# Second attention of a two-layer transformer program: the remainder of the output is subtracted on GpSimd instead of VectorE

## What is computed

```python
q = (x @ wq).reshape(b, s, H, HD); k = ...; v = ...        # H = 32, HD = 16
q = _apply_rotary(q, cos, sin); k = _apply_rotary(k, cos, sin)
scores = jnp.einsum('bqhd,bkhd->bhqk', q, k) * scale
scores = jnp.where(causal[None, None], scores, jnp.finfo(scores.dtype).min)
probs = jax.nn.softmax(scores, axis=-1)
out = jnp.einsum('bhqk,bkhd->bqhd', probs, v).reshape(b, s, d)
return out @ wo
```

## Time and profile before

| | |
|---|---|
| median of three timed runs | 2025.14 us (2019.7 to 2030.21) |
| the profiled execution | 2017.43 us, of it 2015.3 us span |
| TensorE busy | 1927.3 us, 96% of the span |
| VectorE busy | 1525.7 us, 76% |
| ScalarE busy | 882.8 us, 44% |
| GpSimd busy | 885.6 us, 44% |
| second attention, its even course | about 1650 to 1830 us of the span |

### The profile page before, as it was taken

The page is one execution under the profiler, slowest core; times in us unless marked ns, Lnnn a source line. Parts: engine busy times, 40 slices in busy tenths (PEclk is TensorE's granted clock), DMA queues, the critical chain, the costliest instruction groups (busy, mean ns, idle before and its releaser), DMA issues.

```text
span 2015.3 us, 41251 instructions
## 1 busy us (share of the span) xinstructions
PE 1927.3 (96%) x13992; PEld 1685.2 (84%) x13992; DVE 1525.7 (76%) x2354; ACT 882.8 (44%) x2235; POOL 885.6 (44%) x840
## 2 busy tenths in 40 slices
PE   8999979999999999999999999988999989998998
PEld 3688869999999999999999999976889877777776
DVE  2577657787777888777788887877888468778886
ACT  1233334444444444444444444445654445556432
POOL 0123354444444444444444443453685556666111
PEclk9999989999999999999999999999999989999999
DMA  9567751111111111111111111412487754443121
GB/s 336 174 206 240 230 166 47 47 47 47 47 47 47 47 46 44 44 44 45 42 47 47 47 47 42 140 42 63 133 244 222 228 172 127 131 130 98 38 63 58
DMA packets 197085, 207.20 MB, mean 103 GB/s; under 512 B 18554, under 2 KB 167930, under 8 KB 195996
## 3 DMA queue, kind: packets, MB, share of 16 engines
q1 hardware_dynamic: 196156, 205.53, 33.1%
q10 hardware_dynamic: 864, 0.79, 0.1%
HBM read 126.43 MB, written 71.43 MB: 98 GB/s over the span
## 4 chain that ended last, share of the span: by engine, by line
PE 67%; issue 13%; DVE 10%; SPq 3%; POOL 3%; DMA 2%; ACT 1%; DVEq 0%; POOLq 0%; ACTq 0%
PE ps L1028 17%; PE ps L989 17%; PE ps L1003 7%; PE ps L1017 4%; PE ps L1040 4%; SPq L1301 3%; PE ps L1012 3%; PE ps L2543 2%; POOL k_rot L564 2%; DVE f_inv_sum L1984 2%; PE ps L2507 2%; PE ps L1793 2%; PE ps L2114 2%; DVE f_neg_max L1979 2%; PE ps L2085 1%
## 5 line engine op out<-in xcount | busy, mean ns | idle before, releaser
L1028 PE MATMUL ps<-wo,ot 128*128 (+1 forms) x1536 | 388.9, 402 | 0.1
L1028 PEld LDWEIGHTS ps<-wo,ot 128*128 128x128 f32 x1536 | 282.0, 190 | 60.5 <-issue 1.2
L989 PE MATMUL ps<-ht_hi,wq 128*128 (+1 forms) x2048 | 287.5, 283 | 3.9 <-DVE q_swap L862 3.9
L989 PEld LDWEIGHTS ps<-ht_hi,wq 128*128 128x128 f32 x2048 | 268.5, 192 | 9.8 <-DVE q_swap L862 4.1
L789 ACT ACTIVATE prob<-ps,neg_max 128x128 f32<-128x128 f32 (+1 forms) x512 | 208.3, 421 | 130.2 <-DVE neg_max L869 105.2
L946 POOL TENSOR_TENSOR q_rot<-q_rot,q_swap 128x512 f32<-128x512 f32 x128 | 165.1, 1290 | 201.3 <-DVE q_swap L862 196.8
L796 ACT ACTIVATE pt<-ps 128x512 fp32r<-128x512 f32 x192 | 107.9, 598 | 301.7 <-PE ps L1040 301.7
L941 POOL TENSOR_TENSOR prob<-prob,inv_sum 128x512 f32<-128x512 f32 x64 | 66.6, 1040 | 288.2 <-DVE inv_sum L878 288.2
L1979 DVE TENSOR_REDUCE f_neg_max<-ps 128x4 f32<-128x1024 f32 (+1 forms) x128 | 119.7, 954 | 67.1 <-PE ps L2085 60.4
L989 PE MATMUL ps<-ht_lo,wq 128*128 (+1 forms) x1024 | 165.0, 283 | 0.0
L1003 PE MATMUL ps<-pt,vv 128*128 128x512 f32 x576 | 146.0, 397 | 8.6 <-issue 7.7
(11 more groups left out here) (247 smaller groups left out, 4238.0 us busy)
## 6 DMA issues: line engine op xcount, KB each, us to landing
stack_dram<-e_part SPq DMA_DIRECT2D x192, 128.0 KB, 2.4
v_dram<-v_part SPq DMA_DIRECT2D x32, 512.0 KB, 5.6
k_dram<-k_part SPq DMA_DIRECT2D x64, 256.0 KB, 2.7
kk<-k_dram SPq DMA_DIRECT2D x128, 128.0 KB, 2.1
vv<-v_dram SPq DMA_DIRECT2D x128, 128.0 KB, 2.1
wmod<-in_wmod SPq DMA_DIRECT2D x12, 1024.0 KB, 11.5
f_q<-stack_dram SPq DMA_DIRECT2D x62, 192.0 KB, 2.6
f_k<-stack_dram SPq DMA_DIRECT2D x124, 96.0 KB, 2.5
```

What stands on the lines that cost most here:

```text
L989: mm = nc.tensor.matmul(ps_q[j][:, e], w[:, c:c + HD0], r[:, bass.ds(u % B, 1), k].rearrange("p o s -> p (o s)"), start=(n == 0), stop=(n ...
L1028: mm = nc.tensor.matmul(ps_y[j][:], o[:, j, h * P:(h + 1) * P], w[:, bass.ds(at + h * D, D)], start=(n == 0), stop=(n == len(passes) - 1))
```

## The change

The function `low` moves from the program of VectorE to that of GpSimd. On GpSimd it stands behind `cut` and `add_blocks` of the same odd step; on VectorE it stood ahead of `output`. What it waits for and what it announces stay the same, and so do the data.

```diff
@@ -1986,17 +1986,9 @@
             dst = keep.ot1_raw[:, bass.ds(w, 1)].rearrange("p o s -> p (o s)")
             nc.vector.tensor_tensor(dst, ps_o[i][:, 0], inv_sum[i][:], ALU.mult).then_inc(o_out, 1)
 
-        def low(w):
-
-            dve.wait_ge(o_hi, w + 1)
-            hi, lo, raw = (t[:, bass.ds(w, 1)].rearrange("p o s -> p (o s)") for t in (*keep.ot1, keep.ot1_raw))
-            nc.vector.tensor_tensor(lo, raw, f32(hi), ALU.subtract).then_inc(o_split, 1)
-
         def step(v, slot, at):
             if at < U - 2:
                 maxima(v + 2, slot % 2)
-            if 5 <= at and slot % 2:
-                low((v - 5) // 2)
             if 2 <= at and slot % 2:
                 output((v - 3) // 2, (slot + 1) // 2 % 2)
             if at >= TAIL:
@@ -2013,9 +2005,7 @@
             dve.wait_ge(keep.qk_out[n], 192 * B)
         dve.wait_ge(keep.v_kept, 16 * B + 16)
         rest(dve, step)
-        low(PAIRS - 2)
         output(PAIRS - 1, 1)
-        low(PAIRS - 1)
 
     def scalar(act, side):
         def negated(u, slot):
@@ -2066,12 +2056,22 @@
             pool.wait_ge(p_cut, 2 * u + 2)
             nc.gpsimd.tensor_tensor(both[slot % 2][:], prob0[slot % 2][:, :, P:S], prob1[slot % 2][:], ALU.add).then_inc(p_both, 1)
 
+        def low(w):
+
+            pool.wait_ge(o_hi, w + 1)
+            hi, lo, raw = (t[:, bass.ds(w, 1)].rearrange("p o s -> p (o s)") for t in (*keep.ot1, keep.ot1_raw))
+            nc.gpsimd.tensor_tensor(lo, raw, f32(hi), ALU.subtract).then_inc(o_split, 1)
+
         def step(v, slot, at):
             if 0 <= at < U:
                 cut(v, slot)
                 add_blocks(v, slot)
+            if 5 <= at and slot % 2:
+                low((v - 5) // 2)
 
         steps(pool, step)
+        low(PAIRS - 2)
+        low(PAIRS - 1)
 
     def scores(pe, u, slot, at, t):
 
```

## The result

The changed kernel took 2008.04 us in the median of seven runs (1997.66 to 2013.06), the kernel before 2025.14, now the median of seven runs too: ratio 0.991, 95% interval 0.9888 to 0.9932. Predicted were 2009 us and a range of 2001 to 2023. In a later job the ratio came out at 0.992 (0.9906 to 0.9934). The change is faster, by 14 to 23 us by the interval; the forecast was 16.

A forecast was written before the change was run, and what follows sets the result against it. TensorE, busy for 96% of the span, was taken as the bound, so only ending its waits on VectorE pays. Savings of 13.9 + 1.9 + 0.5 = 16.3 us from the 2025.14 us median gave 2009 us, range 2001 to 2023.

The forecast's parts named there:

- part (1): Second attention's loop: VectorE loses 32 remainders, long steps fall to TensorE's own pace of 3.78 us, saving 13.9 us.
- the one free step: First output, taken before any remainder is due: TensorE's step takes 3.79 us without a wait, read as its own pace.
- The margin of 0.16 us: Loop's long step after the change: VectorE's maxima end at 1712.73, TensorE's pace gives 1712.89, so TensorE ends last.
- Part (2): Three pairs that also split weights (g_lo) on VectorE: 0.64 us saved each, 1.9 us in all, bounds 0 to 2.3.
- Part (3): End of the stage, last two remainders leaving VectorE: 0.5 us saved, range -0.3 to 1.2.
- Part (4): GpSimd gains 32 remainders of about 0.74 us behind `add_blocks` in odd steps: cost 0, with 1.7 us of cover.
- Part (5): Loads issued once a step have 0.6 us less time in shorter steps: set at 0, loss up to 0.6.
- rival B: Gain partly given back: TensorE stands longer at the load at 1644, locks at their worst; 9.1 us saved, 2016; chance 0.09.
- Rival A: Freed time runs into the next wait behind VectorE, or run-to-run spread hides the saving; time stays at 2025; chance 0.12.
- Rival C: GpSimd becomes the bound from a remainder of 2.0 us, slower than before from 2.6; 26 us more, 2051; chance 0.04.
- The rule on the exclusive port pair: VectorE with two SBUF inputs and GpSimd block each other for whole instructions; costs 0.13 us a pair with g_lo.
- The rule against elementwise work on GpSimd: Two-input elementwise work belongs on VectorE, GpSimd being about 2 times slower; would cost time only if GpSimd became the bound.

The follow-up runs named there:

- no_remainder: The changed kernel without any remainder of the attention output, the output projection reading the first part instead (timing only): 2009.02 us, ratio 0.991 to the kernel before.
- product_twice: The changed kernel with VectorE's product (L1987) done twice, the second behind the first by a wait: 2018.87 us, ratio 0.996 to the kernel before.
- low_x2: The changed kernel with each remainder on GpSimd done once more into a spare tile: 2007.97 us, ratio 0.9897 to the kernel before.
- low_x3: The changed kernel with two more remainders on GpSimd into a spare tile ahead of each real one: 2013.36 us, ratio 0.9925 to the kernel before.
- low_x4: The changed kernel with three more remainders on GpSimd into a spare tile ahead of each real one: 2038.67 us, ratio 1.0054 to the kernel before.
- changed_again: The changed kernel run once more, unaltered, in a later job beside the kernel with loads in pieces: 2012.91 us, ratio 0.992 to the kernel before.

## Why the prediction was right

- *The bound, and part (1).* Right. Long steps fell from 4.35 and 4.42 to 3.79, not lower, as the one free step said; the loop's 44 steps and the one at 1639 gave 13.5 us where 13.9 were put down. That TensorE ends the step last rests on its being busy for 100 of 100 us and on two runs: no_remainder takes work off GpSimd and doesn't shorten the step, and product_twice puts 0.46 us on VectorE and lengthens it by what exceeds the margin. The margin of 0.16 us was reckoned for the step of 4.42 us from the end of the maxima; but L2094 had started 0.06 us behind that end in the earlier trace rows, which leaves 0.10, and 0.11 was measured there, 0.19 in the other kind.
- *Part (2), the pairs with splits.* Right in mechanism, undersized: 0.81 us each, 2.4 in all, against 0.64 and 1.9, and just outside the bounds of 0 to 2.3. The end of g_lo 0.55 us behind the remainder's end held (0.54 measured). The term that was off is where the remainder stands: it starts 1.38 us after L2094 (1844.53 against 1843.15), where 1.55 was reckoned. The price of the lock itself is 0.38 us a step by no_remainder, larger than the 0.13 in the prediction, since without it g_lo takes 0.68, not 1.09. For the same reason the upper bound was too low: with no remainder at all the step fell by 1.19 us (5.27 to 4.08), 3.6 for three.
- *Part (3), the end.* TensorE reached L2540 22.34 us after the last L2094 instead of 22.65: 0.3 us where 0.5 was taken, out of a range of -0.3 to 1.2. Gain and locks both came, 1.23 us (0.33 ahead of the last reciprocal, 0.90 behind the last product) against 0.93. Of the locks, the one on L2371 had been foreseen (0.49); the 0.44 on the conversion L2458 had not, so that the sum came out near is in part luck.
- *Part (4), GpSimd.* 736 ns for 740; the cut behind it starts 0.88 us after the remainder and nobody waits. Cost 0, shown by low_x2 and low_x3.
- *Part (5), the loads.* Put down as 0; in the two profiles they cost 1.3 us more (the steps from 1618.72 to 1651.97 before take 33.25 us, after 34.00 although 0.55 was saved in them). It is the second stand. It was 1.30 us long before, with a granted clock of 1.00 in the rest of the step, and 1.81 us after, with 0.67. So 0.5 us more of standing went with a step 2.1 us longer, 7.33 for 5.26, while the steps of the first stand got 0.8 shorter. The prediction priced a stand by its length alone and left out the clock behind it. In the nine profiled executions of the changed kernel and of the variants that keep its loads, the second stand took 1.35 to 2.57 us and its step 5.3 to 9.5. That leans towards rival B's mechanism, an earlier TensorE that stands longer, but the kernel before has only one profile, so it was not settled. As a whole B did not come: its 2016 us lie outside the interval.
- *The sum.* Parts (1), (2), (3) and (5) measured 13.5 + 2.4 + 0.3 - 1.3 = 14.9 us in the profiles, against 16.3 forecast; the medians differ by 17.1, and the interval takes in both. With runs of one kernel 15 us apart (1997.66 to 2013.06), that the forecast's 2009 met the median of 2008.04 within 1 us is luck; that the saving is about 15 us is not.
- *Rival A* fell with the trace: nothing stood right behind VectorE. *Rival C* was the right kind of end, and low_x4 brought it about; its 5.6 us for cuts and sums should have been 5.1. Of the sums it said that all 64 take 1.26 to 1.33 us; by line they take up to 1.60, the longest in the last steps beside a g_lo (1862.33 against 1861.67).
- *The rule on the exclusive port pair* (the Trainium skill, page "SBUF — State Buffer", section "SBUF: two separate sides"): the traces agree in the places looked at, with 415 against 822 ns for the same subtraction on VectorE by its place alone, 0.68 against 1.06 us for g_lo, and no change for instructions that read PSUM (products of 424 to 426 ns and reciprocals of 1746 to 1758 in the changed kernel). I had used it for the steps with splits and the end only. Its main lesson was in the loop: half of VectorE's price there was this wait.
- *The rule against elementwise work on GpSimd* (the Trainium skill, page "GPSIMD Engine Reference", section "4.1 Engine selection"): 736 against 415 ns is 1.8 times, so the rule's ratio about holds, and in the loop it cost nothing, since the engine had the time.

## What to carry to other kernels

What moving work off an engine is worth is read from the wait that it ends, and capped by the pace of whoever waits; a step of the same trace that happens to lack the work shows that cap better than any sum. Before moving a two-input instruction off VectorE, look whether it merely stands beside an instruction of GpSimd: here a different place in the same queue gave three quarters of what the other engine gave in the loop (0.45 of 0.60 us a pair). And the largest remaining waste lay beside the tuned loop, in two loads of a megabyte issued just ahead of small ones that were due.

## What was not expected of the hardware

- The same subtraction of 128 x 256 elements on VectorE took 415 ns behind the product and 822 ahead of the reciprocal, though the cut beside it on GpSimd works on another tile. GpSimd is held up likewise: two remainders took 2.33 us beside VectorE's additions, where two of 0.74 would be 1.5. It is not only two-input instructions: the conversion L2458, with one input of 128 x 15 elements, took 0.61 us beside a remainder and 0.17 without.
- Back to back, GpSimd's cuts and sums need no gap: 5.1 us a pair, 1.22 to 1.26 us for two cuts that are 0.63 each.
- A stand of TensorE for loads costs more than its length. In changed_again 5.55 and 2.57 us of stands came with 6.6 us of slower steps: behind the first the granted clock was 0.50, behind the second 0.51, for the rest of the step. Behind the 1.30 us stand of the kernel before it was 1.00. What sets the clock off was not tested.
